# A decoder layer on one core: statistics one step sooner, query blocks in the order 3, 0, 2, 1, and two vector operations moved

## The chip, the core and the metric

The kernel runs on one core of a Trainium2 chip. The core has five engines that run their own instruction streams and wait for each other on semaphores: TensorE (PE: matmuls and transposes, results in PSUM), VectorE (DVE), ScalarE (ACT), GpSimd (POOL) and SyncE (SP, which issues the DMAs here). The metric is the time of one execution in microseconds (us). Lower is better.

## What is computed

For x of 8 sequences of 512 rows by 512 columns, three residual layers follow one another:

```python
x = x + dilated_attention(layernorm(x))        # segments of 128 rows, 16 heads of 32,
                                               # even heads use even rows, odd heads odd rows, q = k = v
x = x + cross_attention(layernorm(x), ctx)     # q = x @ Wq.T, k, v from ctx (512 rows of 128),
                                               # causal softmax(q k / sqrt(32)) v, then @ Wout.T
x = x + mx_ffn(layernorm(x))                   # silu(gate) * up, then down; inputs and weights of
                                               # the three products rounded in blocks of 32 by powers of two
```

## The kernel before

A first block loads and quantises the weights (the first 139 us). Then, for each of B = 8 sequences ("batches"), the work is cut in T = 4 tiles of 128 rows, and runs in two stages. Self-attention of batch 0 stands alone ahead of them; that of batch b + 1 is woven into the feed-forward stage of batch b.

**Cross-attention.** The 16 heads are four column blocks `oc` of four heads. A unit is one column block and one query tile `qt`, 16 units a batch, in the order of the list `units`: qt = 0, 1, 2, 3 inside each oc. Unit qt needs only the keys up to its own diagonal, (qt + 1) * 128 columns, so the units of a block have the sizes 1, 2, 3, 4. For each unit and each pair of heads `pr`, PE computes the scores (`score2`, line 1098, with the causal mask by line 1101), DVE their negated maxima (`maxima`, line 757), ACT the exponentials with their row sums (`exps`, line 952), PE transposes the probabilities (`turn_p2`, line 1115) into PSUM slots C0 and C1, heads 0 and 2 are copied out by DVE (`take_probs`, line 770), heads 1 and 3 by ACT (line 976), and PE multiplies by v (`values2`, line 1136). `recips` on DVE (lines 776 and 779) takes the reciprocals of the row sums and spreads them, `turn_recip` on PE (line 1124) transposes them, ACT copies the result (line 966), and after the last unit of a block `take_out` on DVE (line 785) scales the block's output. The stream of each engine is software-pipelined by hand. In step u:

- PE: first scores of unit u + 1; `turn_recip` and `values2` of u - 1; in one step of a block the query projection of the next block (`project_q`, 12 matmuls, line 526); transposes of heads 0 and 1 of u; second scores of u + 1; transposes of heads 2 and 3; in one step the key projection `project_k`. In the last block the output product (line 1152) begins in the place of the projections.
- ACT: copy of `turn_recip` of u - 1; first exps of u + 1; in two steps `take_k` (line 940) or `take_q` (line 932); its two copies of probabilities; second exps of u + 1.
- DVE: first maxima of u + 1; first copy; in one step `take_out`; second maxima of u + 1; second copy; `recips(u)`.

A slot is written again only when the copy of what stood in it is done: head 2 waits in C0 for DVE's first copy, head 3 in C1 for ACT's first copy, `turn_recip` in C1 for ACT's second, and `values2` for the copies of heads 2 and 3.

**Feed-forward.** Twenty-one steps i. In steps 0 to 15 PE computes gate and up (line 1176), ACT the silu (line 990), DVE the product, block maxima and scales (`gated`, lines 833, 807, 810, 840, 841), POOL scales the product down (line 691), DVE clips it (`round_inter` of step i - 1, line 803, called q below), POOL scales it back (line 691 again), PE transposes it (line 1187) and adds the down product (line 1198), which DVE takes out after every fourth (`take_down`, line 850). `quantise_x` and `round_x` prepare the next tile.

**Self-attention, woven in.** Tile t has four parts, in steps 4t + 1 to 4t + 4. Part 0: PE transposes the normalised tile xn1 (line 634), ACT copies it, DVE computes `shift2` of tile t - 1 (line 513) and ACT the second normalisation of t - 1 (line 519). Part 1: PE scores (line 642), ACT exps (line 616). Part 2: v and the output (lines 526 and 652); DVE sums, reciprocals and scaling (lines 566, 568, 575), then the statistics of tile t + 1 (`moments_of`, lines 495 to 497); POOL adds the residual (line 541), then computes 1/sqrt (`power`, line 503) of t + 1. Part 3: DVE waits for that and normalises tile t + 1 (line 508), then takes the second statistics of tile t.

All engines work strictly in the order in which this code issues.

## Time and profile before

| | before |
|---|---|
| median of 3 runs | 1723.53 us (1723.16 to 1724.51) |
| the profiled execution: its own time, its span | 1723.65 us, 1721.9 us |
| PE busy, share of the span | 1390.1 us, 81% |
| DVE busy | 1140.8 us, 66% |
| ACT busy | 857.4 us, 50% |
| POOL busy | 547.4 us, 32% |
| mean granted clock of PE | 0.972 |

In the profile's rows a time is the start in us from the start of the span, then follow the duration, the engine, the line, the operation with the names of output and input, the shapes and a count; a bracket at the end is the time in which the engine stood idle before the row, and what ended it. Rows of one engine can overlap a little, since its instructions are pipelined; what a group costs is best read from its start to the start of the next. "issue" is idle time with no wait behind it. In a table of windows each stretch gives its length and then, for each engine, the busy time with the number of instructions, the granted clock of PE (1.00 is 2.4 GHz), the DMA share and GB/s. In a table of waits the columns are total, number and longest.

### The profile page before, as it was taken

The page shows a single profiled execution, that of the slowest core. Times are in us where ns is not written, and L with a number is a line of the kernel's source. Part 1 is how long each engine was busy: PE and PEld are TensorE (multiplying, and loading weights), DVE is VectorE, ACT ScalarE, POOL GpSimd, SP SyncE. Part 2 cuts the span into 40 slices and gives each one's busy share as a digit, 9 for nine tenths or more (in the row PEclk, how much of TensorE's full clock was granted, in tenths as well). Part 3 has the DMA queues.
Part 4 walks back from the last instruction along what each step waited for, and adds up shares of the span by engine and source line. Part 5 has one row for each costly group of instructions (what it writes and reads, how often), then busy time and mean ns, then how long its engine had stood idle before and what let it go on. Part 6 is the DMA issues. An engine that isn't in the chain of part 4 may idle for free.

```text
span 1721.9 us, 31184 instructions
## 1 busy us (share of the span) xinstructions
PE 1390.1 (81%) x11267; PEld 803.6 (47%) x11344; DVE 1140.8 (66%) x2475; ACT 857.4 (50%) x2098; POOL 547.4 (32%) x494
## 2 busy tenths in 40 slices
PE   1223899789988899889988899889988899889987
PEld 0112554445544554445544554455544554455533
DVE  8994455874578555874578555865578556865576
ACT  2442464456634564456634564456634664456622
POOL 5882000650046200650046200650046101640055
PEclk9999999989998999999999999999999999999998
DMA  5311000000000000000010000000000000000001
GB/s 189 110 55 37 1 2 15 18 13 14 2 26 14 19 1 21 13 13 14 2 26 13 19 1 26 7 20 7 2 26 13 19 1 26 7 20 1 2 1 25
DMA packets 25285, 36.07 MB, mean 21 GB/s; under 512 B 2480, under 2 KB 10672, under 8 KB 25136
## 3 DMA queue, kind: packets, MB, share of 16 engines
q1 hardware_dynamic: 25136, 34.09, 7.3%
q8 instruction: 93, 1.52, 0.4%
q14 instruction: 56, 0.46, 0.1%
HBM read 25.69 MB, written 8.39 MB: 20 GB/s over the span
## 4 chain that ended last, share of the span: by engine, by line
PE 43%; DVE 29%; ACT 9%; issue 8%; POOL 2%; DMA 0%; SPq 0%; ACTq 0%; DVEq 0%; POOLq 0%
PE psum L1098 9%; PE psum L526 7%; PE psum L1115 7%; DVE top L807 5%; PE psum L1136 5%; DVE inter L833 4%; PE psum L1152 3%; PE psum L1101 3%; DVE nmx L757 2%; PE psum L1198 2%; DVE q L803 2%; PE psum L1176 2%; ACT silu L990 2%; DVE stats L495 2%; DVE top L810 2%
## 5 line engine op out<-in xcount | busy, mean ns | idle before, releaser
L757 DVE TENSOR_REDUCE nmx<-psum 128x2 f32<-128x256 f32 (+3 forms) x256 | 210.9, 824 | 184.5 <-PE psum L1101 182.5
L503 POOL TENSOR_TENSOR rstd<-var_eps,minus_half 128x1 f32<-128x1 f32 x96 | 59.8, 623 | 828.9 <-DVE var_eps L497 828.7
L952 ACT ACTIVATE p<-psum,nmx 128x384 f32<-128x384 f32 (+3 forms) x512 | 265.9, 527 | 67.4 <-DVE nmx L757 60.9
L770 DVE COPY pt<-psum 128x128 f32<-128x128 f32 (+3 forms) x256 | 124.5, 486 | 145.4 <-PE psum L1115 145.0
L1115 PE MATMUL psum<-ident,p 128*128 128x128 f32 x1280 | 198.3, 280 | 26.1 <-ACT pt L976 22.8
L691 POOL TENSOR_TENSOR inter<-inter,rscale 128x512 f32<-128x512 f32 x128 | 141.3, 1104 | 207.7 <-DVE rscale L841 206.5
L1098 PE MATMUL psum<-k_f,q_f 32*128 32x128 f32 (+3 forms) x1024 | 206.9, 480 | 0.6
L976 ACT COPY pt<-psum 128x128 f32<-128x128 f32 (+3 forms) x256 | 109.2, 426 | 139.5 <-PE psum L1115 138.1
L1198 PE MATMUL psum<-wd_sb,iq_t 128*128 128x512 bf16 x483 | 140.4, 406 | 42.0 <-DVE x_res L850 30.6
L1115 PEld LDWEIGHTS psum<-ident,p 128*128 128x128 f32 x1280 | 137.2, 140 | 61.1 <-ACT pt L976 33.4
L1176 PE MATMUL psum<-wg_sb,xq_t 128*128 128x512 bf16 x504 | 140.2, 403 | 6.5 <-DVE inter L833 6.5
L691 POOL TENSOR_TENSOR iq<-q,scale 128x512 bf16<-128x512 fp8e4 x128 | 142.8, 1115 | 0.4 <-DVE q L803 0.4
L833 DVE TENSOR_TENSOR inter<-psum,silu 128x512 f32<-128x512 f32 x128 | 86.6, 677 | 83.6 <-ACT silu L990 83.0
L1176 PE MATMUL psum<-wu_sb,xq_t 128*128 128x512 bf16 x510 | 137.9, 394 | 0.1
L990 ACT ACTIVATE silu<-psum 128x512 f32<-128x512 f32 x128 | 76.0, 593 | 114.4 <-PE psum L1176 114.1
L1152 PE MATMUL psum<-wo_sb,xn 128*128 128x512 f32 x256 | 114.6, 596 | 6.5 <-DVE xn L785 6.5
L427 PE MATMUL psum<-ident_b,w_q 128*128 128x128 bf16 x192 | 26.3, 309 | 112.2 <-POOL w_q L334 108.1
L998 ACT COPY iq_t<-psum 128x512 bf16<-128x512 bf16 x128 | 74.5, 582 | 84.1 <-PE psum L1187 84.1
L1098 PEld LDWEIGHTS psum<-k_f,q_f 32*128 32x128 f32 x1024 | 76.8, 183 | 57.0 <-issue 48.5
L952 ACT ACTIVATION_READ_ACCUMULATOR p<-psum,nmx 128x1 f32 x512 | 103.0, 201 | 0.0
L526 PE MATMUL psum<-x_t,wq_hl 128*128 128x512 f32 (+1 forms) x480 | 99.9, 357 | 0.3
L1198 PEld LDWEIGHTS psum<-wd_sb,iq_t 128*128 128x128 bf16 x512 | 49.4, 103 | 106.7 <-issue 43.5
(104 smaller groups left out, 2421.4 us busy)
## 6 DMA issues: line engine op xcount, KB each, us to landing
x_in<-in_x_dram SPq DMA_DIRECT2D x32, 256.0 KB, 4.0
out_dram<-x_res SPq DMA_DIRECT2D x64, 128.0 KB, 2.4
w_raw<-in_w_gate_dram SPq DMA_DIRECT2D x16, 256.0 KB, 2.7
w_raw<-in_w_up_dram SPq DMA_DIRECT2D x16, 256.0 KB, 3.1
w_raw<-in_w_down_dram SPq DMA_DIRECT2D x16, 256.0 KB, 3.6
ctx_in<-in_ctx_t_dram SPq DMA_DIRECT2D x8, 256.0 KB, 2.9
wq_raw<-in_wq_t_dram SPq DMA_DIRECT2D x1, 1024.0 KB, 7.8
wo_sb<-in_wo_t_dram SPq DMA_DIRECT2D x1, 1024.0 KB, 10.0
```

The source lines that it names most:

```text
L526: last = pe.matmul(dst, w, x, start=(n == 0), stop=(stop and n == len(terms) - 1))
L691: pool.tensor_tensor(dst.rearrange("p (n k) -> p n k", k=BLOCK), src.rearrange("p (n k) -> p n k", k=BLOCK), scales.unsqueeze(2).to_broadc ...
L757: dve.tensor_reduce(nmx2[:, u % UNITS, 2 * pr:2 * pr + 2], where(("scores2", oc, qt, pr))[:, :, 0:(qt + 1) * P], AX_X, ALU.max, negate=Tru ...
L770: free(dve.tensor_copy(pt2[:, hh, 0:m], where(label)[:, 0, 0:m]), label)
L833: free(dve.tensor_tensor(inter[:, r, :], where(label)[:, 1, :], silu[:, i % 2, :], ALU.mult), label)
L952: ins = act.activation(p2[:, (4 * u + hh) % P2_RING, 0:m], where(label)[:, hh % 2, 0:m], ACT.Exp, bias=nmx2[:, u % UNITS, hh:hh + 1], accu ...
L990: act.activation(silu[:, i % 2, :], where(label)[:, 0, :], ACT.Silu).then_inc(S["silu_ready"], 1)
L1098: pe.matmul(where(label)[:, j, 0:m], q_f[rows, oc % 2, qt * P:(qt + 1) * P], k_f[rows, oc % 2, 0:m], start=True, stop=False)
L1115: last = pe.transpose(where(label)[:, 0, kt * P:(kt + 1) * P], p2[:, (4 * u + hh) % P2_RING, kt * P:(kt + 1) * P], ident[:])
L1152: last = pe.matmul(where(label)[:, 0, :], out_n[:, oc, t % T * P:(t % T + 1) * P], wo_sb[:, oc, :], start=(oc == 0), stop=(oc == OC - 1))
L1176: last = pe.matmul(where(label)[:, j, :], xq_t[:, t % 2, c * P:(c + 1) * P], w[:, c, m * CH:(m + 1) * CH], start=(c == 0), stop=(c == C - 1))
L1198: last = pe.matmul(where(label)[:, 0, :], iq_t[:, i % RING, j * P:(j + 1) * P], wd_sb[:, 4 * m + j, :], start=(m == 0 and j == 0), stop=(m ...
```

## The change

1. **Query blocks.** `QT_ORDER = (3, 0, 2, 1)` takes the place of 0, 1, 2, 3 in the list of units and in the plan of PSUM slots. What was tied to a tile (k and q projections and their copies, `take_out`, the first parts of the output product) is tied to the place in the order.
2. **Reciprocals.** `recips(u)` moves from the end of DVE's step to behind the first copy of probabilities, ahead of `take_out`, the second maxima and the second copy.
3. **Statistics of self-attention.** On DVE `moments_of` of tile t + 1 moves from the end of part 2 to part 1, and its normalisation from part 3 to the head of part 2. POOL's `power` of tile t + 1 moves from part 2 to part 1.
4. **Down product.** `take_down` moves ahead of `round_inter` in its step.

```diff
+QT_ORDER = (3, 0, 2, 1)
...
-            for qt in range(T):
+            for qt in QT_ORDER:
...
-            if part == 2 and 0 <= t < T - 1:
+            if part == 1 and 0 <= t < T - 1:
                 power(pool, 1, g + 1)
...
+            if part == 1 and 0 <= t < T - 1:
+                dve.wait_ge(x_loaded[(t + 1) // 2], 32 * (b + 1))
+                moments_of(dve, link, x_in[:, t + 1, :], 1, g + 1)
+            if part == 2 and 0 <= t < T - 1:
+                dve.wait_ge(S["rstd1_ready"], g + 2)
+                normalise(dve, xn1[:, (t + 1) % 2, :], x_in[:, t + 1, :], 1, g + 1).then_inc(S["xn1_ready"], 1)
             if part == 2 and 0 <= t < T:
...
-            if part == 2 and 0 <= t < T - 1:
-                dve.wait_ge(x_loaded[(t + 1) // 2], 32 * (b + 1))
-                moments_of(dve, link, x_in[:, t + 1, :], 1, g + 1)
-            if part == 3 and 0 <= t < T - 1:
-                dve.wait_ge(S["rstd1_ready"], g + 2)
-                normalise(dve, xn1[:, (t + 1) % 2, :], x_in[:, t + 1, :], 1, g + 1).then_inc(S["xn1_ready"], 1)
...
                         take_probs(u, 0)
-                        if qt == 0 and oc % OC:
+                        recips(u)
+                        if place[qt] == 0 and oc % OC:
                             take_out(oc - 1)
                         if u + 1 < end:
                             maxima(u + 1, 1)
                         take_probs(u, 1)
-                        recips(u)
...
                             gated(b * CHUNKS + i)
+                        if i % 4 == 3 and i > 4:
+                            take_down(b * T + i // 4 - 1)
                         if 1 <= i <= CHUNKS:
                             round_inter(b * CHUNKS + i - 1)
...
-                        if i % 4 == 3 and i > 4:
-                            take_down(b * T + i // 4 - 1)
...
-                        if qt == 1 and more:
+                        if place[qt] == 1 and more:
                             take_k(oc + 1)
-                        if qt == 2 and more:
+                        if place[qt] == 2 and more:
                             take_q(oc + 1)
...
-                        if qt == 2 and more:
+                        if place[qt] == 2 and more:
                             project_q(oc + 1)
...
-                        if qt == 0 and more:
+                        if place[qt] == 0 and more:
                             project_k(oc + 1)
-                        if not more and 0 < qt < 3:
+                        if not more and 0 < place[qt] < 3:
 
-                            output(b * T, [0, 1] if qt == 1 else [2])
+                            output(b * T, [0, 1] if place[qt] == 1 else [2])
```

No operation is added or removed, and no shape is changed.

## Rows read from the trace of the kernel before

**Rows 1.** Windows: a block, the last block, the start of cross-attention, part of feed-forward.

```profile
597.35:618.92 21.57, 19.93 (x192) 12.50 (x188) 11.91 (x26) 13.72 (x46) 0.00 (x0) 1.00 0.00 1
...
651.21:673.35 22.14, 19.54 (x201) 10.88 (x200) 12.46 (x27) 13.27 (x43) 0.00 (x0) 1.00 0.00 1
584.78:590.82 6.04, 5.33 (x36) 2.84 (x36) 2.93 (x8) 4.51 (x17) 0.00 (x0) 1.00 0.06 21
...
684.00:757.00 73.00, 61.75 (x500) 32.69 (x507) 60.79 (x152) 34.83 (x54) 46.10 (x46) 0.95 0.07 15
```

**Rows 2.** Waits of PE in the cross-attention of one batch, 584.7 to 673.4.

```profile
PE psum L1124 <- DVE recip_x L779: 4.1, 6, 0.9
PE psum L1115 <- ACT pt L976: 2.8, 4, 0.7
```

**Rows 3.** Timeline around the reciprocals of unit qt = 2.

```profile
600.96 1.13 PE L1098 MATMUL psum<-k_f,q_f 32*128 32x512 f32 x4
...
602.14 0.82 PE L1115 MATMUL psum<-ident,p 128*128 128x128 f32 x6
602.34 1.22 DVE L757 TENSOR_REDUCE nmx<-psum 128x2 f32<-128x1024 f32 x1 [1.04 <-PE psum L1101]
...
602.89 0.49 PE L1098 MATMUL psum<-k_f,q_f 32*128 32x128 f32 x4
...
603.48 0.55 DVE L770 COPY pt<-psum 128x384 f32<-128x384 f32 x1
...
604.52 0.30 PE L1124 MATMUL psum<-ident,recip_x 128*128 128x128 f32 x1 [0.92 <-DVE recip_x L779]
...
604.75 0.86 PE L1136 MATMUL psum<-pt,v_sb 128*32 128x128 f32 x24
...
605.54 1.09 PE L1115 MATMUL psum<-ident,p 128*128 128x128 f32 x8
```

**Rows 4.** Timeline of the step with the copy of k, unit qt = 1.

```profile
612.39 0.91 PE L1098 MATMUL psum<-k_f,q_f 32*128 32x384 f32 x4
...
614.55 0.58 ACT L952 ACTIVATE p<-psum,nmx 128x384 f32<-128x384 f32 x1 [0.61 <-DVE nmx L757]
...
615.67 0.58 ACT L940 COPY k_f<-psum 128x512 f32<-128x512 f32 x1
...
616.14 0.39 ACT L976 COPY pt<-psum 128x256 f32<-128x256 f32 x1
...
616.59 0.44 PE L1115 MATMUL psum<-ident,p 128*128 128x128 f32 x2 [0.72 <-ACT pt L976]
```

**Rows 5.** Timeline of self-attention alone, batch 0.

```profile
163.01 0.98 ACT L616 ACTIVATE e<-psum,self_shift 128x256 f32<-128x256 f32 x2 [0.48 <-PE psum L642]
...
167.15 0.86 DVE L575 TENSOR_TENSOR tmp<-psum,rcp 64x256 f32<-64x256 f32 x2 [2.13 <-PE psum L652]
...
188.28 0.86 DVE L575 TENSOR_TENSOR tmp<-psum,rcp 64x256 f32<-64x256 f32 x2 [2.13 <-PE psum L652]
...
192.48 0.81 ACT L519 ACTIVATE xn<-x_in,shift,rstd 128x512 f32<-128x512 f32 x1 [0.69 <-DVE shift L513]
```

**Rows 6.** Timeline of feed-forward with self-attention, tile t = 2.

```profile
734.95 1.00 DVE L513 SCALAR_TENSOR_TENSOR shift<-moments,rstd 128x1 f32<-128x1 f32 x1
...
741.85 0.69 DVE L833 TENSOR_TENSOR inter<-psum,silu 128x512 f32<-128x512 f32 x1 [2.14 <-ACT silu L990]
...
744.04 1.10 POOL L691 TENSOR_TENSOR inter<-inter,rscale 128x512 f32<-128x512 f32 x1 [2.43 <-DVE rscale L841]
...
746.59 0.69 DVE L495 BATCH_NORM_STATS2 stats<-x_in 128x6 f32<-128x512 f32 x1
...
750.03 1.26 DVE L508 TENSOR_SCALAR xn<-x_in,moments,rstd 128x512 f32<-128x512 f32 x1
```

**Rows 7.** Timeline at the end of the last batch: POOL and DVE together.

```profile
1708.15 1.04 POOL L691 TENSOR_TENSOR iq<-q,scale 128x512 bf16<-128x512 fp8e4 x1
1708.22 1.25 DVE L803 TENSOR_SCALAR q<-inter 128x512 fp8e4<-128x512 f32 x1 [0.34 <-POOL inter L691]
```

More of the change, by code:

```diff
@@ L456, in decoder_layer @@
         nc.all_engine_barrier()
-        units = [(oc, qt) for oc in range(B * OC) for qt in range(T)]
+        units = [(oc, qt) for oc in range(B * OC) for qt in QT_ORDER]
+        place = {qt: n for n, qt in enumerate(QT_ORDER)}
+        LAST_QT = QT_ORDER[-1]
         UNITS = OC * T
@@ L465, in until_values @@
             oc, qt = units[u]
-            if qt == T - 1:
+            if qt == LAST_QT:
                 until_filled(eng, ("outT", oc))
             else:
-                eng.wait_ge(S["values_done"], (T - 1) * oc + qt + 1)
+                eng.wait_ge(S["values_done"], (T - 1) * oc + place[qt] + 1)
         P1_STEPS = 4 * T + 5
@@ L929, in take_q @@
                     if oc >= 2:
-                        until_filled(act, ("scores2", oc - 2, T - 1, 1))
+                        until_filled(act, ("scores2", oc - 2, LAST_QT, 1))
                     free(act.mul(q_f[:, oc % 2, :], where(label)[:, 0, :], SCALE), label)
@@ L936, in take_k @@
                     if oc >= 2:
-                        until_filled(act, ("scores2", oc - 2, T - 1, 1))
+                        until_filled(act, ("scores2", oc - 2, LAST_QT, 1))
                     until_filled(act, label)
@@ L963, in take_recip @@
                     until_filled(act, label)
-                    if oc and qt == 0:
+                    if oc and place[qt] == 0:
                         until_freed(act, ("outT", oc - 1))
@@ L1090, in score2 @@
                     m = (qt + 1) * P
-                    if qt == 0 and pr == 0:
+                    if place[qt] == 0 and pr == 0:
                         until_freed(pe, ("k", oc))
@@ L1127, in values2 @@
                     oc, qt = units[u]
-                    if qt == 0:
+                    if place[qt] == 0:
                         until_free(pe, ("outT", oc))
@@ L1139, in values2 @@
                                              start=(kt == 0), stop=(kt == qt))
-                    if qt == T - 1:
+                    if qt == LAST_QT:
                         fill_done(last, ("outT", oc))
```

2 lines of the change are left out of this document (1 added, 1 removed).

## The prediction

> **What bounds the kernel now.** I read first the windows of single stages [rows 1], then PE's waits in one batch of cross-attention [rows 2], and then the timelines around them. Cross-attention is PE's stage: in a full block PE is busy 19.93 of 21.57 us, at the full clock, while DVE and ACT have 12 and 14 us of work. What PE loses there are two waits in every block, one for DVE's reciprocals and one for ACT's copy of probabilities: 4.1 and 2.8 us a batch. The weave of feed-forward and self-attention is DVE's: 60.79 of 73 us, with POOL at 46 us beside it; most of the 12 us left is DVE waiting for a silu that ACT gives late, because ACT itself waits for `shift2` and then loads its tables around the exps [rows 6]. Self-attention of batch 0 is bound by no engine; it is one chain of latencies. So each part of the change has to be read against another bound: on DVE work in the same order of size costs nothing while PE leads, and costs all of itself in the weave.
>
> **Self-attention alone.** Today a tile takes half of 188.28 - 167.15 us, 10.56 [rows 5], because PE may transpose the next tile only when DVE has, behind its scaling of this one, made the statistics and the normalisation of the next. After the change both are finished long before PE is free. What is late next is the second normalisation, since ACT issues it ahead of the exps: scaling (188.28) to the end of ACT's normalisation (193.2) is 4.9 us, exps (163.01) to the next scaling (167.15) is 4.14. That is a period of 9.1 us, and with three periods the gain is 3 x 1.46 = 4.4 us. Above it can't go without shortening this second chain; if PE's transposes were late for another reason, the gain would be 0. I take 4.4.
>
> **Reciprocals and query order, a full block.** The first wait: from the second scores of the big unit (600.96) to the transposed reciprocals (604.52) are 3.56 us [rows 3]. PE has 2.47 us of its own to do in between: scores 1.18, six transposes 0.75, scores of the small unit 0.54 (1.18 less the 0.64 by which its row is shorter). So 1.09 us are lost, and the chain that costs them is scores to maxima 1.38, maxima 1.14, copy of head 2 with the reciprocals behind it 1.04. With `recips` ahead of the maxima this wait disappears, but `values2` of the same unit still waits for the copy of head 2, which stands behind the same maxima: 1.38 + 1.14 + a copy of 256 columns, about 0.4 (384 take 0.55), and 0.06 to PE, 3.0 us. PE's own work up to there is now 1.18 + 0.55 (four transposes) + 0.54 + 0.23 (604.52 to 604.75) = 2.5. So 0.5 us stays of 1.09.
>
> The second wait: from the scores (612.39) to head 3 (616.59) are 4.20 us [rows 4]: maxima, two exps, the copy of k, then ACT's copy of head 1, for which slot C1 is held. The bracket says 0.72 idle; from start to start, without the modelled ends, PE's own work there is about 3.3, so 0.9 is lost. In the new order the same step has the same next unit (qt = 2) and the same copy of k, but its own unit is qt = 0: the copy is 0.13 shorter, three fewer transposes save PE 0.35, and `values2` is that of qt = 3, 24 matmuls more, about 0.7 (605.54 - 604.75 is 0.79 for 24). The wait becomes 4.07 - 3.65 = 0.4. I walked the other steps in the same way. Two small new waits show: ACT's first copy in the step of qt = 1 stands behind two exps of 512 columns (0.1 us), and the copy of the transposed reciprocals behind the next two (0.1 to 0.2). `take_out`, now 0.4 later on DVE and behind a copy of 512 columns, still ends about when PE wants its slot for k: its cover is nearly used up, and every 0.1 us more would be PE's. The waits of a block go from 2.0 to 1.2 us, 0.8 less, and three blocks of a batch have the projections: 2.4 us.
>
> **Start and end of a batch.** The first unit is now qt = 3. Its two score groups take 2.36 us in place of 1.1, its maxima end 2.6 us after the start, its first two exps at 4.0, and only then is the slot free for the next scores; PE, with its filling matmuls, is done at 3.2. It waits 0.85 us, against about 1.1 now (6.04 us for 5.0 us of work, start to start; the window's own idle is 0.7 [rows 1]). The longer matmuls are work that the batch has anyway. At the end nothing is left to cover the waits: the last block has 22.14 us with 19.54 busy, start to start some 3.5 us lost. The last unit is now qt = 1, so that between its last transpose and the output product stand a copy of 256 and 16 matmuls, not a copy of 512 and 32. Walked through, 1.8 us are lost, 1.7 less. A batch gains 2.4 + 0.25 + 1.7 = 4.35 us. A walk overlooks small waits rather than adding some; for 16 steps I take off 0.03 each, which gives 3.9, and for 8 batches **31.2 us**. Bounds: nothing, if each wait removed comes back as another, and 6.9 us a batch, if both of [rows 2] go with nothing in their place.
>
> **The weave, 7 batches.** From `shift2` (734.95) to the product of part 2 (741.85) are 6.90 us, set by ACT, and DVE waits 2.14 us of them [rows 6]. The statistics of the next tile, from 746.59 about 1.1 us to the next product, now lie in this wait, for tiles t = 1 and t = 2. For t = 0 there is no such wait (no `shift2` goes ahead of it), and they only change places. Against this stands what POOL does to DVE. A q that asked 0.07 us after POOL's start took 1.25 us [rows 7], not 0.36, and the normalisation at 750.03, just behind POOL's start, 1.26 us. Three consequences. (a) `take_down` ahead of q (0.69 long like line 833's, the same shape) lets POOL's scaling, 1.10 us from 744.04, begin first; q then waits for its end: 0.6 us more in parts 2 of t = 1, 2 and 3. (b) The normalisation of t + 1 follows that late q at once, ahead of POOL's next operation, and so takes 0.6 us less for t = 1, 2; for t = 0, where no `take_down` is, it waits as now. (c) In part 3 the second statistics move up to where the normalisation was, and end just as POOL goes on; the normalisation of `quantise_x` behind them, free today, now comes about 0.07 us late and waits, 0.6 us more for t = 0 and 1. Sum: t = 0 +0.6; t = 1 -1.1 - 0.6 + 0.6 + 0.6, that is -0.6 with rounding; t = 2 -1.2; and for t = 3 the late q puts the last residual, and behind it the second normalisation on ACT and the query projection, 0.5 later. That is -0.7 us a batch, **-4.9 us** for seven. Bounds: all of (a) and (c) fall away, 3.9 us a batch; or no wait is filled and all hit, +3 us a batch.
>
> The Trainium skill, "SBUF — State Buffer", section "Who interferes with whom", has the rule that speaks against edit 4: VectorE in a two-port mode and GpSimd share one pair of ports, and whoever comes first holds it for its whole instruction, while a VectorE instruction with one SBUF input outside these modes doesn't contend. By that rule q pays the 0.6 us behind `take_down`, and `take_down` itself pays nothing; the trace agrees as far as it goes (1.25 against 0.36 us for one q). Without the rule the weave would give 3.9 us a batch.
>
> In the last batch, with no self-attention, q costs 0.6 us once on DVE's path, and `take_down` gives PE 0.3 us back at two places: 0. POOL's `power`, moved up a part, waits for statistics that are ready before its next scaling is asked for: 0. No DMA and nothing on SP is moved.
>
> **Sum.** 1723.65 of the profiled execution (0.1 above the median) - 4.4 - 31.2 - 4.9 = 1683.1 us.
>
> **Rivals.** *The waits come back.* DVE's second maxima and ACT's exps are where they were; if `values2` or a slot waits as long as the reciprocals did, a batch gains 1.5 us: 1723.65 - 4.4 - 12 - 4.9 = 1702. For it: PE's wait in [rows 3] ends only 0.6 us behind one that stays. Against it: PE has more of its own work between. 0.18.
> *No port waits in the weave.* 27 us there in place of 4.9: 1661. For it: (c) hangs on 0.07 us. Against it: [rows 7] is that very distance. 0.10.
> *Slower, by POOL.* Eleven short operations a batch stand at a new distance to POOL's: three normalisations, three q, two of `quantise_x`, three of the statistics. If each waits for a whole operation, 0.9 us, seven batches pay 69 us and the sum is 1757. It decides from six of the eleven on (35.6 us of gains are 5.1 a batch). For it: DVE leads there. Against it: three of them wait already [rows 6], and the statistics have the wait of [rows 6] around them. 0.04.
> *It does nothing.* PE's idle time in cross-attention is only an artefact of modelled ends, and the weave eats the first gain: 1722. 0.03.
> The forecast itself has 0.65.
>
> **Range.** From 1663, most of the way to the third case, to 1707, which holds the second with its spread. It leaves out the slower case, no change, and a part of the case without port waits. A run of this kernel can tell 0.2%, 3.4 us. Faster: 0.65 + 0.18 + 0.10 = 0.93; within 0.2%: 0.03; slower: 0.04.
>
> **What would show it.** In the profile after: periods of 9.1 us in the first self-attention; 20.8 us from one key projection to the next; no waits of PE for the spread reciprocals, 0.5 for the copy of head 2, 0.4 for ACT's copy next to the copy of k; 84.7 us from the first scores to the output product, in place of 88.6; q of 0.9 us or more behind `take_down`, a normalisation of 0.5 us behind it. Wrong it would be made by a wait of PE for the slot of the next k, or by a q that POOL holds longer than one operation.

## The result and the profile after

| | before, beside it | after |
|---|---|---|
| median | 1724.02 us (4 runs, 1723.16 to 1724.69) | 1673.76 us (4 runs, 1672.65 to 1677.77) |
| ratio, with 95% interval | | 0.9716 [0.9702, 0.9729] |
| the profiled execution: time, span | 1723.65 us, 1721.9 us | 1672.65 us, 1670.9 us |

The change saves 50 us, 2.8%. 1683.1 with a range of 1663 to 1707 was predicted: the direction and the range held, the gain was put 10 us too small. Behind line 41 the line numbers of the kernel after are 1 to 3 higher, and those of L566 to L575, behind a part that was moved, 10 (L1098 is L1101, L1115 is L1118, L1124 is L1127, L1136 is L1139, L803 is L806, L850 is L853).

**Where the 51.0 us of span went.** I cut both executions at four marks that the order of the work leaves alone: the load of x, the first gate matmul of each batch, the first query projection of each weave, and the end.

```
                                             before    after   difference
weights, to the first load of x              139.66   136.37      -3.3
batch 0: self- and cross-attention, output   159.90   150.89      -9.0
weave, mean of 7                              87.40    86.64   7 x -0.76 = -5.3
cross-attention and output, mean of 7        105.49   100.99   7 x -4.50 = -31.5
last feed-forward                             72.09    70.27      -1.8
```

Groups of instructions by line, with the idle time before them behind the last bar; these are PE's transposes of probabilities, before and after the change:

```profile
L1115 PE MATMUL psum<-ident,p 128*128 128x128 f32 x1280 | 198.3, 280 | 26.1 <-ACT pt L976 22.8 <-DVE pt L770 2.8
```

```profile
L1118 PE MATMUL psum<-ident,p 128*128 128x128 f32 x1280 | 204.8, 281 | 12.7 <-ACT pt L979 6.9
```

The number of transposes (1280) and the mean time of one (280 and 281 ns) are unchanged; they waited 26.1 us in the whole span before, and wait 12.7 now.

**Self-attention alone.** Its period, read on PE's product for v in the timeline after:

```profile
158.94 1.65 PE L529 MATMUL psum<-wkv_hl,ctx_hl 128*128 128x512 f32 x3 [2.12 <-ACT e L619]
...
167.97 1.65 PE L529 MATMUL psum<-wkv_hl,ctx_hl 128*128 128x512 f32 x3 [2.11 <-ACT e L619]
```

9.03 us against 10.56 [rows 5], where 9.1 was forecast. What PE waits for is now ACT's exps, as the prediction had it: the normalisation ahead of them is the chain that is left.

**Cross-attention.** The windows after answer to [rows 1]: a block (from one query projection to the next), and a batch from its first scores to the output product. Beneath them are PE's waits in that batch; the table of [rows 2] showed 4.1 and 2.8 us.

```profile
599.85:620.51 20.66, 20.10 (x189) 12.50 (x188) 11.81 (x26) 13.76 (x47) 0.00 (x0) 1.00 0.01 2
565.46:649.52 84.06, 80.16 (x743) 48.50 (x743) 47.72 (x100) 55.56 (x184) 0.00 (x0) 1.00 0.01 3
```

```profile
PE psum L1118 <- ACT pt L979: 0.9, 3, 0.3
PE psum L1155 <- DVE xn L788: 0.8, 1, 0.8
PE psum L1101 <- ACT p L955: 0.7, 1, 0.7
PE psum L1127 <- ACT pt L979: 0.5, 1, 0.5
PE psum L1118 <- DVE pt L773: 0.3, 1, 0.3
```

The wait for the spread reciprocals is gone, as forecast, and nothing of its size took its place. The one new row is the 0.7 us in front of the scores, at the start of a batch, where PE waits for the first exps. The timeline after of the step with the copy of k, and of the step in which `values2` should wait for the copy of head 2:

```profile
614.77 0.92 PE L1101 MATMUL psum<-k_f,q_f 32*128 32x384 f32 x4
...
618.06 0.58 ACT L943 COPY k_f<-psum 128x512 f32<-128x512 f32 x1
...
618.52 0.28 ACT L979 COPY pt<-psum 128x128 f32<-128x128 f32 x1
...
618.86 0.33 PE L1118 MATMUL psum<-ident,p 128*128 128x128 f32 x1 [0.29 <-ACT pt L979]
...
628.34 1.13 PE L1101 MATMUL psum<-k_f,q_f 32*128 32x512 f32 x4
...
629.52 0.89 PE L1118 MATMUL psum<-ident,p 128*128 128x128 f32 x4
...
629.72 1.23 DVE L760 TENSOR_REDUCE nmx<-psum 128x2 f32<-128x1024 f32 x1 [0.72 <-PE psum L1104]
...
630.86 0.42 DVE L773 COPY pt<-psum 128x256 f32<-128x256 f32 x1
...
630.89 0.32 PE L1127 MATMUL psum<-ident,recip_x 128*128 128x128 f32 x1
...
631.33 0.65 PE L1139 MATMUL psum<-pt,v_sb 128*32 128x128 f32 x16
```

Both waits have the size that was forecast, if they are read as the prediction read them, from start to start. The first: from the scores (614.77) to head 3 (618.86) are 4.09 us, where a chain of 4.07 with 0.4 lost was put; the bracket says 0.29, and it said 0.72 where 0.9 was lost before [rows 4]. The second: from the second scores (628.34) to the values (631.33) are 2.99 us, where 3.0 with 0.5 lost was put. No bracket shows that loss, because it lies in two places. The values begin 0.44 us behind the transposed reciprocals and elsewhere 0.21 (619.87 to 620.08, for instance); and the four transposes ahead of it take 0.82 us to the next scores, where 0.55 was put: the third starts at 629.98, just behind the end of ScalarE's copy (629.92).

**The weave.** DVE's timeline after, tiles t = 1 and t = 2:

```profile
690.28 1.00 DVE L516 SCALAR_TENSOR_TENSOR shift<-moments,rstd 128x1 f32<-128x1 f32 x1
...
697.18 0.69 DVE L836 TENSOR_TENSOR inter<-psum,silu 128x512 f32<-128x512 f32 x1
...
699.21 0.63 DVE L853 TENSOR_TENSOR x_res<-psum,x_res 128x512 f32<-128x512 f32 x1
699.76 0.95 DVE L806 TENSOR_SCALAR q<-inter 128x512 fp8e4<-128x512 f32 x1
700.62 0.53 DVE L511 TENSOR_SCALAR xn<-x_in,moments,rstd 128x512 f32<-128x512 f32 x1
...
706.25 1.25 DVE L511 TENSOR_SCALAR x_f<-x_res,moments,rstd 128x512 f32<-128x512 f32 x1
...
711.09 1.00 DVE L516 SCALAR_TENSOR_TENSOR shift<-moments,rstd 128x1 f32<-128x1 f32 x1
...
718.00 0.69 DVE L836 TENSOR_TENSOR inter<-psum,silu 128x512 f32<-128x512 f32 x1 [1.14 <-ACT silu L993]
...
729.36 1.00 DVE L516 SCALAR_TENSOR_TENSOR shift<-moments,rstd 128x1 f32<-128x1 f32 x1
```

The same two stretches between two `shift2` before:

```profile
713.52 1.00 DVE L513 SCALAR_TENSOR_TENSOR shift<-moments,rstd 128x1 f32<-128x1 f32 x1
...
754.53 1.00 DVE L513 SCALAR_TENSOR_TENSOR shift<-moments,rstd 128x1 f32<-128x1 f32 x1
```

Each of the three effects is there. The q behind `take_down` takes 0.95 us, the normalisation behind it 0.53, the normalisation of `quantise_x` 1.25. The wait for silu in part 2 was 1.14 us for t = 1 (at 720.42 in the timeline before) and 2.14 for t = 2 [rows 6]; it is filled for t = 1 (697.18 has none) and 1.14 for t = 2. From one `shift2` to the next are 20.81 and 18.27 us; before they were 21.43 and 19.58 (713.52, then 734.95 [rows 6], then 754.53).

The weave as a whole is another matter. Up to its last product on DVE it is 74.03 us long in every batch, and was 75.37 in six of seven (75.99 in one). From there to the next batch's first query projection there are two lengths, with two granted clocks. Here are two weaves before, then the one after from which the rows above come:

```profile
761.42:772.87 11.45, 7.69 (x46) 5.13 (x48) 8.09 (x19) 5.92 (x11) 5.16 (x5) 0.85 0.11 24
953.71:966.28 12.57, 8.80 (x46) 5.64 (x48) 8.09 (x19) 6.03 (x11) 5.16 (x5) 0.73 0.11 23
```

```profile
736.26:748.82 12.56, 8.93 (x47) 5.58 (x48) 8.62 (x19) 6.01 (x11) 5.14 (x5) 0.73 0.10 22
```

Before, four of seven ends took 11.4 to 11.6 us and three 12.5 to 12.6; after the change all seven take 12.3 to 12.7. So of the 1.4 us that a weave gains up to the last product, 0.7 is given back behind it, where the clock stays low for longer.

### The profile page after: what moved, and what is told of

The parts are those of the page before. It is cut to its first block, busy times and chain, and to the rows that moved or that the text cites. A ratio compares the mean times of both kernels' runs of the same rounds, so it can differ in the third digit from the quotient of the medians.

```text
span 1670.9 us, 31184 instructions
## 1 busy us (share of the span) xinstructions
PE 1385.5 (83%) x11267; PEld 802.3 (48%) x11344; DVE 1147.6 (69%) x2475; ACT 854.8 (51%) x2098; POOL 547.2 (33%) x494
## 4 chain that ended last, share of the span: by engine, by line
PE 41%; DVE 31%; ACT 11%; issue 6%; POOL 2%; DMA 0%; SPq 0%; ACTq 0%; POOLq 0%; DVEq 0%
PE psum L1101 9%; PE psum L1118 8%; PE psum L529 7%; DVE top L810 6%; PE psum L1139 4%; DVE inter L836 4%; PE psum L1155 4%; DVE q L806 3%; PE psum L1104 3%; ACT p L955 3%; DVE nmx L760 2%; ACT silu L993 2%; DVE top L813 2%; DVE x_f L511 2%; DVE tmp L585 2%
## 5 line engine op out<-in xcount | busy, mean ns | idle before, releaser
L760 DVE TENSOR_REDUCE nmx<-psum 128x2 f32<-128x1024 f32 (+3 forms) x256 | 210.7, 823 | 167.3 <-PE psum L1104 166.6
L1118 PE MATMUL psum<-ident,p 128*128 128x128 f32 x1280 | 204.8, 281 | 12.7 <-ACT pt L979 6.9
L773 DVE COPY pt<-psum 128x512 f32<-128x512 f32 (+3 forms) x256 | 124.7, 487 | 129.1 <-PE psum L1118 127.5
L1101 PE MATMUL psum<-k_f,q_f 32*128 32x512 f32 (+3 forms) x1024 | 206.8, 480 | 5.8 <-ACT p L955 5.3
L1201 PE MATMUL psum<-wd_sb,iq_t 128*128 128x512 bf16 x483 | 147.9, 425 | 74.3 <-ACT iq_t L1001 44.6
L1118 PEld LDWEIGHTS psum<-ident,p 128*128 128x128 f32 x1280 | 138.7, 140 | 53.6 <-issue 19.0
L979 ACT COPY pt<-psum 128x512 f32<-128x512 f32 (+3 forms) x256 | 109.3, 427 | 97.7 <-PE psum L1118 95.5
L1179 PE MATMUL psum<-wg_sb,xq_t 128*128 128x512 bf16 x504 | 130.0, 380 | 19.2 <-DVE inter L836 19.2
L836 DVE TENSOR_TENSOR inter<-psum,silu 128x512 f32<-128x512 f32 x128 | 86.6, 677 | 68.2 <-ACT silu L993 66.6
L1179 PE MATMUL psum<-wu_sb,xq_t 128*128 128x512 bf16 x510 | 131.1, 379 | 0.1
L1101 PEld LDWEIGHTS psum<-k_f,q_f 32*128 32x128 f32 x1024 | 76.8, 183 | 61.7 <-issue 43.1
```

The source lines that it names most:

```text
L760: dve.tensor_reduce(nmx2[:, u % UNITS, 2 * pr:2 * pr + 2], where(("scores2", oc, qt, pr))[:, :, 0:(qt + 1) * P], AX_X, ALU.max, negate=Tru ...
L773: free(dve.tensor_copy(pt2[:, hh, 0:m], where(label)[:, 0, 0:m]), label)
L836: free(dve.tensor_tensor(inter[:, r, :], where(label)[:, 1, :], silu[:, i % 2, :], ALU.mult), label)
L1101: pe.matmul(where(label)[:, j, 0:m], q_f[rows, oc % 2, qt * P:(qt + 1) * P], k_f[rows, oc % 2, 0:m], start=True, stop=False)
L1118: last = pe.transpose(where(label)[:, 0, kt * P:(kt + 1) * P], p2[:, (4 * u + hh) % P2_RING, kt * P:(kt + 1) * P], ident[:])
L1179: last = pe.matmul(where(label)[:, j, :], xq_t[:, t % 2, c * P:(c + 1) * P], w[:, c, m * CH:(m + 1) * CH], start=(c == 0), stop=(c == C - 1))
```

## Experiments

Ratios are to the kernel before in the same job, with the 95% interval. In the table of stages "attention" is cross-attention and output, "rest" what batch 0 has between the load of x and its first gate matmul.

```
                            time us   ratio                      weights   rest  attention  weave    last
order of blocks alone       1723.42   1.0002 [0.9990, 1.0015]     139.8   159.7   105.85    87.17   71.3
reciprocals alone           1707.14   0.9907 [0.9890, 0.9924]     139.4   159.6   103.28    87.78   72.0
order and reciprocals       1684.69   0.9776 [0.9762, 0.9791]     136.2   157.1   100.99    87.18   73.0
statistics alone            1707.78   0.9908 [0.9893, 0.9923]     139.9   155.6   105.50    85.71   73.1
take_down alone             1734.71   1.0055 [1.0041, 1.0069]     140.1   160.9   105.74    89.01   69.4
after, take_down late       1665.48   0.9656 [0.9642, 0.9669]     136.9   152.9   100.97    85.14   74.0
... early in last batch     1664.84   0.9648 [0.9634, 0.9661]     139.5   151.6   100.97    85.16   68.9
order, gap filled           1708.70   0.9909 [0.9895, 0.9922]     138.9   158.8   103.76    87.43   70.3
... and k behind the copy   1659.71   0.9625 [0.9607, 0.9643]     139.9   150.1    99.88    85.71   70.6
after, once more            1676.31   0.9729 [0.9712, 0.9747]     139.0   150.9   100.97    86.58   70.3
... and tail filled         1656.38   0.9613 [0.9594, 0.9632]     139.5   151.3    99.87    85.06   69.0
```

The lines that begin with dots build on the version "take_down late": early in the last batch, then k behind the copy, then the filled tail.

**The order of blocks alone** (edit 1, all else as before).

```diff
-QT_ORDER = (0, 1, 2, 3)
+QT_ORDER = (3, 0, 2, 1)
```

> Only the new order of query blocks (edit 1). Theory (the gains of edits 1 and 2 add up, since each shortens another wait): the wait for the reciprocals stays near 1 us a block, the one beside the copy of k shrinks to 0.3 to 0.4, and the end of a batch is shorter; cross-attention gains 1.9 us a batch, 15 us in all, 1709 us. Rival (the order by itself is worth nothing, the reciprocals do it all): within 3 us of before. Second rival (the order does it all): 1688.

The median did not move, and by the number alone the theory had fallen. The stages say otherwise. In three of the seven batches attention and output take 103.57 us, 1.9 less than before; in three others they take 108.3, and in the first 105.3. The same two stretches as windows, and PE's timeline where the slow one loses its time:

```profile
580.26:683.83 103.57, 96.94 (x805) 57.41 (x806) 57.30 (x123) 56.92 (x187) 4.20 (x5) 1.00 0.05 11
770.85:879.13 108.28, 101.66 (x804) 60.16 (x805) 57.60 (x122) 56.89 (x187) 4.20 (x5) 0.95 0.05 11
```

```profile
798.06 0.89 PE L1118 MATMUL psum<-ident,p 128*128 128x128 f32 x4
...
798.88 0.49 PE L1101 MATMUL psum<-k_f,q_f 32*128 32x128 f32 x4
...
800.31 0.36 PE L1127 MATMUL psum<-ident,recip_x 128*128 128x128 f32 x1 [0.72 <-DVE recip_x L782]
...
801.61 1.97 PE L1118 MATMUL psum<-ident,p 128*128 128x128 f32 x8
```

Eight transposes take 1.97 us here and 1.04 one block before (779.75): the array ran at its 1.2 GHz level. The granted clock was 0.65 over the 4 us from 801, and 1.00 in the faster batch. Ahead of the fall PE had stood idle for 0.72 us, behind a short group of scores and in front of the transpose of the reciprocals. The same gap (0.73 us, at 863.04) also stands 1.7 us ahead of this batch's output products, and the stretch from them to the next gate matmul takes 14.4 instead of 12.7 us. So the order alone gains 1.9 us a batch and gives it back in clock. That the gap takes the clock down was only argued at this point; the run with the gap filled tests it.

**Reciprocals alone** (edit 2).

```diff
                         take_probs(u, 0)
+                        recips(u)
...
                         take_probs(u, 1)
-                        recips(u)
```

> Only the reciprocals behind the first copy (edit 2), query blocks in the order 0 to 3. Theory: of 1.09 us in each of three blocks 0.43 stays, as values2 waits for the copy of head 2 behind the maxima; with 0.7 us at the end of a batch that is 2.7 us a batch, 21 us in all, 1702. Rival (the waits come back one for one): less than 12 us gained. Second rival (the reciprocals do it all): 1688.

A batch gains 2.2 us (105.49 to 103.28), a block 0.40 (the query projections start at 403.32, 424.49 and 445.67: 21.17 us). The expectation was 5 us too good.

**Order and reciprocals** (edits 1 and 2).

> Edits 1 and 2 together, without the edits to self-attention and to take_down. Theory: 4.48 us a batch as in the profile of the changed kernel, 36 us in all, 1688; the weave keeps its lengths of before. Rival: if part of what the cross-attention gained came from the statistics (data ready earlier), this is more than 3 us slower than 1688.

1684.7, 3.3 us less than expected. The profiled execution has the short weight stage (below), 3.5 us less than before; of the other three no profile says which they had. A batch is at 100.99 us, exactly that of the full change: the statistics and `take_down` have no part in cross-attention. The two edits gain 1.9 and 2.2 us a batch alone and 4.5 together.

**Statistics alone** (edit 3).

```diff
-            if part == 2 and 0 <= t < T - 1:
+            if part == 1 and 0 <= t < T - 1:
                 power(pool, 1, g + 1)
...
```

> Only the statistics of self-attention one step sooner (edit 3). Theory: 4.6 us in the first self-attention, in each of seven weaves the wait of 2.14 us is filled for two tiles, less 0.6 us of port wait for two normalisations: 1.1 us each, together 12 us, 1712. If the weight stage is 3.3 us shorter in this kernel too, its profile shows the first w_pow at 0.9 us and not at 3.5, and the time is 1709. Rival (the port waits eat the weave's gain): 1719.

The weave falls by 1.69 us, more than I had for it and more than it falls in the full change (0.76): 2.2 us less up to the last product (73.19 us), and behind it all seven ends are of the long kind (12.5 to 12.7 us). The rest of the batch-0 stage gives the 4.3 us of self-attention.

**take_down alone** (edit 4).

```diff
+                        if i % 4 == 3 and i > 4:
+                            take_down(b * T + i // 4 - 1)
                         if 1 <= i <= CHUNKS:
                             round_inter(b * CHUNKS + i - 1)
...
-                        if i % 4 == 3 and i > 4:
-                            take_down(b * T + i // 4 - 1)
```

> Only the residual (take_down) goes ahead of the rounding in its step; everything else is as before. My theory: in seven weaves this costs and gives nothing back. It puts about 0.63 us (the residual) in front of the q8 rounding three times a weave, and the whole lap of DVE and POOL grows by a part of that; the change with the residual left late is the next run, and the statistics alone gave weaves of 85.9 us where the full change has 86.8, so I put the edit at 0.9 to 1.6 us a weave, 6 to 11 us in seven. The last batch, where no self-attention stands behind the residual, should win some 0.3 to 0.6 us. Sum: 1730 to 1735 us, some +8 to before, weaves of 88.5 to 89 us. Rival one (that was my own sum's assumption, that the residual early costs only what it delays in the first step and is given back at the end of the step): within 2 us of before, weaves of 87.6 us in the mean. Rival two (early residuals free DVE for the next batch's steps, and the statistics' gain of 1.6 a weave is only held back by something else): 1718 or less.

Slower by 0.55%, 10.4 us between the medians: the weave is 1.6 us longer, 1.0 of them ahead of the last product. This edit is a loss by itself. One of its seven batches shows the fall of the clock in the old order of blocks too: its attention and output take 107.18 us and the others 105.5, all of it in the output stage, 14.4 instead of 12.7 us.

**The full change with take_down late.**

> The full change, but the residual is where it was before, behind the rounding and the statistics of its step. If the residual early costs 0.9 us a weave (weaves of 86.8 us in the full change, 85.9 with the statistics alone), the seven weaves are 85.9 us here, 6 us less in all, the last batch gives back 0.3 to 0.6, and the time is 1667 to 1669 us, a ratio to before of 0.968 to 0.969 against the 0.9716 of the full change. Rival: the difference between 86.8 and 85.9 comes from the order of the cross-attention blocks and from where its reciprocals end, not from the residual; then the weaves stay at 86.8 us and the time within 1.5 us of 1673.8.

The weave falls from 86.6 to 85.1 us. The timeline of this version shows why, at the place of 699.21 above:

```profile
699.03 0.36 DVE L806 TENSOR_SCALAR q<-inter 128x512 fp8e4<-128x512 f32 x1
699.31 0.68 DVE L853 TENSOR_TENSOR x_res<-psum,x_res 128x512 f32<-128x512 f32 x1
699.90 0.67 DVE L511 TENSOR_SCALAR xn<-x_in,moments,rstd 128x512 f32<-128x512 f32 x1
```

Here q gets ahead of POOL's next multiplication and takes 0.36 us; the residual lies beside that multiplication, and the normalisation needs 0.67. With the residual first, q pays 0.95 and the normalisation 0.53, and the product behind them comes 0.41 us later, twice in a weave (5.74 us behind the one before it, not 5.33). Up to the last product that makes 0.8 us of the 1.5. The rest lies behind it, where four ends take 12.3 to 12.4 us and three 11.3 to 11.5: again the two kinds. The version gains more than I expected, 8 us on the full change (10.8 beside its repetition), though its profiled last stage was the longest of all, 74.0 us.

**The same, take_down early in the last batch.**

> As the run before it, but in the last batch, where no self-attention follows, the residual goes ahead of the rounding as in the full change. Theory: it ends 0.3 to 0.6 us sooner than the run before it, at 1667 to 1668 us: the last residual is the last but one instruction of the program, and there it no longer stands behind a rounding. Rival: the last down projections end at the clock's lower level in one and not in the other, and that is worth more (up to 1.5 us) than the place of the residual; then the two differ by over 1 us either way and their last batches differ in the granted clock.

The medians differ by 0.6 us, within their spread: the rival's difference of over 1 us is not there, and the theory's 0.3 to 0.6 can't be told from none. The profiled last stages differ by 5 us, and the windows of their ends (the first version's, then this one's) show the granted clock that the rival had named:

```profile
1650.00:1666.50 16.50, 8.81 (x28) 3.27 (x28) 3.37 (x7) 1.75 (x3) 3.15 (x3) 0.53 0.15 32
```

```profile
1651.50:1662.90 11.40, 4.80 (x28) 2.17 (x28) 2.30 (x4) 1.76 (x3) 3.16 (x3) 0.94 0.22 46
```

From the start of the last four down products to the end of the last it is 10.9 us in the first and 6.8 in the second, 4.0 of the 5 us; the other 1.0 lies ahead of them.

**The order alone, with PE busy in the gap.** Three matmuls on operands that are already loaded stand in front of one transpose of reciprocals in each block (the trace holds two of each three). They take no wait away.

```diff
                     until_free(pe, label)
+                    for _ in range(3 if units[u][1] == 1 else 0):
+                        pe.matmul(where(label)[:, 0, :], ident_b[:], wd_sb[:, 0, :], start=True, stop=True)
                     pe.wait_ge(S["rx_ready"], u + 1)
```

> The other order of query blocks alone, as in the first run of this study, which came out at 1723.4 us, no faster than before, though its undisturbed blocks were 21.33 us instead of 21.57 and its batches 90.5 instead of 92.4. Here three matmuls of 128x512 on operands already loaded (0.21 us each) are put in front of the one reciprocal transpose of each block that PE waits for (0.72 us of idle time in front of it), so PE is busy in that gap; the transpose itself can start no sooner. They add work and take no wait away. My theory: that gap of 0.7 us, right behind other short waits, is what lets the granted clock fall to its 1.2 GHz level (0.50) for a few microseconds in some blocks and in the output stage (blocks of 22.8 us, output stages of 14.56 us instead of 12.87), and this ate the gain. Then, with the gap filled, there are no stretches with a clock of 0.50 inside the cross-attention, the output stages are all 12.87 us, and the time is 1707 to 1713 us. Rival: the clock falls for another reason (the waits of 0.3 us for the copies, or the mix of small matmuls of the new order); then stretches at 0.50 stay, and the time is 1722 us or more, up to 3 us above the first run if the matmuls are in the way.

Adding work makes the kernel 14.7 us faster. All seven batches take 103.73 to 103.80 us, none is slow, and the windows of the two batches that stand above at 1.00 and 0.95 are both at 1.00:

```profile
576.44:680.17 103.73, 99.12 (x812) 58.21 (x817) 57.23 (x122) 56.84 (x187) 4.19 (x5) 1.00 0.05 11
767.46:871.20 103.74, 99.15 (x812) 58.24 (x817) 57.55 (x123) 56.83 (x187) 4.22 (x5) 1.00 0.05 11
```

```profile
605.25 0.59 PE L1127 MATMUL psum<-wd_sb,ident_b 128*128 128x512 bf16 x2
605.83 0.33 PE L1129 MATMUL psum<-ident,recip_x 128*128 128x128 f32 x1
```

With work in the idle gap the clock stays up, in an order of blocks that is otherwise the same: so without this gap there is no fall, and the lower clock is where the order's gain had gone. That the idle time and not too little work over a longer stretch is the cause is not shown, since no run put the same matmuls elsewhere. The gap is not enough by itself: the kernel before has gaps of 0.92 us [rows 3] and keeps 1.00 in cross-attention, and with `take_down` alone, in that same old order, one batch of seven has the fall. What else must be there stays open.

The Trainium skill, "TensorE: Matmul & The Clock Gate", section "A second HAM failure mode: psum-queue depth-cycling", describes a kernel of another kind in which PE's frequent short idle times between groups of matmuls, while it cycles through PSUM, make the clock swing between its two levels. The two runs agree as far as that idle times of 0.72 us are followed by a swing between these levels; here they are waits for a result of VectorE, and no run shows whether it matters how frequent they are.

**k behind ScalarE's first copy.** It takes away the 0.29 us at 618.86.

```diff
-                        if place[qt] == 1 and more:
-                            take_k(oc + 1)
-                        if place[qt] == 2 and more:
-                            take_q(oc + 1)
                         take_probs(u, 0)
+                        if place[qt] == 1 and more:
+                            take_k(oc + 1)
+                        if place[qt] == 2 and more:
+                            take_q(oc + 1)
```

> The version before it (full change, residual late in all batches but the last, 1664.8 us), and ScalarE copies the next block's k and scaled q behind its first copy of transposed probabilities instead of ahead of it. In the full change TensorE waits 0.29 us for that copy once a block, next to ScalarE's copy of k, in three of four blocks. Theory: this wait goes and nothing takes its place, 0.25 to 0.3 us in 24 blocks: 6 to 7 us less, 1658 to 1659 us, blocks of 20.4 us instead of 20.67. Rival: the copy of k (0.5 us and more) now stands in front of the second copy of probabilities and of the exponentials behind it, TensorE waits there instead, and blocks are 20.7 to 21.2 us, the time 1664 to 1677 us.

The median falls by 5.1 us, to 1659.71, where 6 to 7 less was expected; blocks are 20.3 us long, 20.4 was expected. That is 1.1 us a batch, between the sum of the three waits by their brackets (0.9) and from start to start (1.3), and no new wait: of the five rows of the full change four are left in PE's table of waits of a batch (its lines 1103, 1120, 1129 and 1157 are 1101, 1118, 1127 and 1155 there).

```profile
PE psum L1157 <- DVE xn L788: 0.8, 1, 0.8
PE psum L1103 <- ACT p L957: 0.7, 1, 0.7
PE psum L1129 <- ACT pt L981: 0.5, 1, 0.5
PE psum L1120 <- DVE pt L773: 0.3, 1, 0.3
```

**The full change once more.**

> The full change once more, unchanged, beside the versions built on it. The profiled execution of it that I have read has a weight stage 3.3 us shorter than the one of before, because its first pass over the scaled weights (w_pow) took 0.90 us instead of 3.51: VectorE's instruction started 0.16 us ahead of GpSimd's second multiplication there and not behind it. Theory: this is decided anew in each execution by when the first weights arrive, it is no part of the change. Then the median is within 2 us of 1673.8, and whether this profile's w_pow takes 0.9 or 3.5 us, the rest of its span (all behind the first load of x) is within 1 us of the first one's 1534.5 us (1670.9 less 136.4), but for the last four down projections, where the granted clock may differ. Rival: the change (its new start of the program) always gives the short weight stage; then w_pow is 0.9 here, and was 0.9 in all versions with the new statistics and 3.5 in all without; the versions run so far already speak against it.

The median is 2.6 us above the first one, just outside the 2 us that I had given. From the load of x to the end the span is 1534.1 us, against 1534.5. The weight stage is where the two profiles part. The first two rows are of the first profile, the third is of this one:

```profile
11.13 0.90 DVE L379 TENSOR_SCALAR w_pow<-w_y 128x1536 int32<-128x1536 int32 x1
...
11.29 3.36 POOL L328 TENSOR_TENSOR w_y<-w_raw,w_r 128x1536 f32<-128x1536 f32 x1 [0.37 <-DVE w_r L372]
```

```profile
11.22 3.52 DVE L379 TENSOR_SCALAR w_pow<-w_y 128x1536 int32<-128x1536 int32 x1
```

One instruction, 2.6 us apart. In the short case DVE starts it 0.16 us ahead of POOL's second multiplication; in the long one POOL is first. Of the thirteen profiles here three are short (0.90 to 0.96 us) and ten long (3.51 to 3.54); the full change has one of each. The 3.3 us of the first comparison are therefore no part of the change. The arrival of the first weights, which the expectation named, does not decide it: DVE's first reduction starts at 5.94 us in a short profile and at 5.93 in a long one. What the three short profiles have, and none of the ten long, is a wait of DVE's second reduction for its DMA (0.20 to 0.49 us). It puts the reciprocals, and behind them POOL's second multiplication, later than `w_pow`. In the first profile of the change:

```profile
8.48 1.75 DVE L358 TENSOR_REDUCE w_top<-w_raw 128x48 f32<-128x1536 f32 x1 [0.49 <-DMA w_raw<-in_w_down_dram]
```

**The tail filled.** In the last batch matmuls on loaded operands stand ahead of the last four down products, in a PSUM slot that is no longer used.

```diff
+                        if b + 1 == B and i >= CHUNKS:
+                            idle = ("recipT", B * OC - 1, LAST_QT)
+                            until_freed(pe, idle)
+                            for _ in range(9 if i == CHUNKS else 4):
+                                pe.matmul(where(idle)[:, 0, :], ident_b[:], wd_sb[:, 0, :], start=True, stop=True)
                         if INTER_LAG < i <= CHUNKS + INTER_LAG:
```

> The first version of this group, with matmuls of 128x512 on operands already loaded (0.21 us each) in front of the last four down projections, in a part of PSUM that nothing uses by then: nine ahead of the first of the four, where TensorE waits 2.4 to 2.7 us for VectorE, four ahead of each of the others, where it waits 0.7. Theory: TensorE's idle time there is what takes the granted clock to its lower level (0.53 to 0.58 in the last 15 us of two profiles, where four matmuls of the down projection take 1.86 to 1.89 us; 0.94 in a third, 1.04 us). With the gaps filled they always take 1.04 us. The fillers are in the way by at most 0.1 us each time. The median is 1 to 3 us less than the first version's, and its runs lie closer together. Rival: the clock does not fall for idle time but by the work done before; then its level is as often low here, and the fillers, themselves twice as long at the lower level, hold the projections up: equal or up to 3 us more.

3.3 us less in the median than the version without the fillers, a little beyond the forecast; the runs don't lie closer together (1651.9 to 1659.2, against 1655.8 to 1661.5). Not all of it can be the fillers' doing. Of the 5.4 us between the two profiled spans 1.6 are in the last stage; 4.5 are in the seven weaves, which the edit doesn't touch (85.71 and 85.06 us in the mean). The first two of the four down products took 1.81 and 1.30 us without the fillers (all four 1.86 to 1.89 in the version with `take_down` late); here they are all at the upper level, of which the first and the last:

```profile
1643.39 1.02 PE L1203 MATMUL psum<-wd_sb,iq_t 128*128 128x512 bf16 x4 [0.45 <-DVE x_res L853]
...
1649.23 1.03 PE L1203 MATMUL psum<-wd_sb,iq_t 128*128 128x512 bf16 x4
```

But they were also at the upper level, 1.02 to 1.04 us, in the version with `take_down` early in the last batch, which has no fillers. So one profile doesn't show that the fillers hold the clock up. This is the best version of the study: 1656.38 us, a ratio of 0.9613, 17 to 20 us under the full change.

## Why the prediction was right, and where its sizes were off

- **Self-attention alone**, 4.4 us: measured 4.6 (3 x (10.56 - 9.03)), with ACT's normalisation as the next thing late. Right.
- **Cross-attention**, 31.2 us: measured 36.0 (8 x 4.50). The walk itself had said 4.35 a batch; the 0.03 us a step that I took off ("A walk overlooks small waits rather than adding some") was the mis-sized term, 3.6 of the 4.8 us. Inside the walk, three blocks gave 2.7 us (21.57 to 20.67 each) where 2.4 was put; the two waits of a block that were forecast, 0.5 and 0.4 us from start to start, have their sizes, and which small wait was put 0.1 too large is not known; start and end of a batch gave the rest, 88.54 - 84.06 - 2.7 = 1.8, where 1.95 was put. `take_out`, whose cover was called nearly used up, held nobody.
- **The weave**, 4.9 us: measured 5.3. The tiles come out as worked out: t = 0 0.58 us longer where 0.6 was put, t = 1 0.62 shorter where 0.6 was put, t = 2 1.31 where 1.2 was put. What was put for t = 3, 0.5 longer, came in at 0.7 by another way, and there the sum is right partly by luck: the end of the weave is one of two lengths, 1.1 us apart, with a granted clock of 0.85 or 0.73, and the change has the long one in all seven weaves where before three had it. In the one weave whose rows are compared above (the third) the gain is 0.23 us, not 0.7. No run here was made to tell what decides between the two. The split was less right: effect (b), a normalisation of 0.53 us behind the late q, was booked as a credit of `take_down`. But without the early residual the normalisation stands behind the residual and takes 0.67, not 1.26. The credit belongs to the statistics, and `take_down` costs 1.5 us a weave: 0.41 at each of two late q, and 0.7 at the end of the weave, where the third late q and the clock are not told apart. Edit 3 alone is worth 1.7.
- **Last batch and weights**, 0: measured 1.8 and 3.3 us in this pair of profiles. The first is the granted clock of the last four down products (9.8 us from the start of the first to the end of the last before, 8.1 after). Whether it comes with the change is open: in the thirteen profiles the last stage is 68.9 to 70.6 us where `take_down` is early in the last batch, and 70.3 to 74.0 where it is late, but no run was made for it and the medians of the two versions that differ in this alone are 0.6 us apart. The second is the start of one DVE instruction and not the change's doing; the repetition of the full change has the long weight stage and a span of 1673.1.
- **What is left to explain.** 1683.1 less 4.8 (cross-attention), 0.2 and 0.4 (self-attention, weave), 3.3 and 1.8 is 1672.6; the profiled time was 1672.65.
- **The rivals.** *The waits come back*: they did not, the table of waits has none of that size. *No port waits in the weave*: each of the three was there, 0.95, 1.25 and 1.27 us. *Slower, by POOL*: of the eleven short operations those that were named waited, and no others. What none of the rivals had is the clock: the order of blocks alone gives its 15 us back through it. The full change has no such fall in cross-attention, and no such gap, because the reciprocals were moved with it. That was not foreseen: a prediction for the order alone from the same walk would have been wrong by 14 us, as the first expectation was. That the edits were made together is luck.

The rule of the Trainium skill, "SBUF — State Buffer", section "Who interferes with whom", that a VectorE instruction in a two-port mode waits for all of a GpSimd instruction that came first, agrees with the trace in both directions: q and normalisations at 0.95 to 1.27 us, the residual from PSUM at 0.63 us and undisturbed, and `w_pow` at 3.5 us when POOL is first and 0.9 when it is not, where POOL's multiplication takes 3.36 us instead of 2.77.

## What to carry to other kernels

Split a change that bundles several moves before you keep it: here one of four moves was a loss of 1.5 us in each of seven stages, hidden in the gain of another. When a version with less waiting is not faster, look at the granted clock of single stages before you drop the idea; behind a gap of 0.7 us the lost clock can cost more than the gap, and cheap work put into it can pay. And before a difference of a few microseconds is explained, look whether it lies in a stage that the edit touches.

## What was not expected of the hardware

- With the other order alone, gaps of 0.72 us in front of one transpose were followed by PE at its 1.2 GHz level (eight transposes 1.97 us, not 1.04; the output stage 14.4, not 12.7 us). With matmuls in the gap it stayed at 2.4 GHz. The kernel before has longer gaps, of 0.92 us, without a fall; its cross-attention with `take_down` moved has one fall in seven batches.
- The last four down products took 1.02 to 1.89 us each from one version to the next, by the clock alone; in the profile before three of the four were at the lower level, in that with `take_down` late all four, and none with fillers ahead of them, nor in the version without fillers that has `take_down` early in the last batch alone.
- The end of a weave, from DVE's last product to the next query projection, takes 11.3 to 12.0 us at a granted clock of 0.85 or 0.86, or 12.1 to 12.9 at 0.72 or 0.73, in 89 of the 91 weaves of the thirteen profiles, and in most versions both in one execution, with the same code.
- A VectorE instruction with one result per row, `shift2`, takes 1.00 us in the weave where it meets POOL and 0.16 where it doesn't (744.88 in the timeline after).
